# VectorE adds the scaled down product to the rows in four feed-forward units, in place of GpSimd, with the five engines' orders written anew behind the head

## The reference

```python
x = x + 0.5 * L0_ffn(layernorm(x))      # 704 hidden, integer weights with scales s_gate, s_up, s_down, silu
x = x + L0_attn(layernorm(x))           # 16 heads of 16, rotary, causal
x = x + 0.5 * L0_ffn(layernorm(x))
x = x + 0.5 * L1_ffn(layernorm(x))      # ternary weights, sigmoid gate
x = x + L1_attn(layernorm(x))           # 16 query heads, 4 key heads, linear position bias, causal
x = x + 0.5 * L1_ffn(layernorm(x))
```

## Time and profile before

| | us |
|---|---|
| median of 3 runs (lowest, highest) | 552.77 (552.47, 553.46) |
| the profiled execution | 552.14 |
| its span, first to last instruction | 550.4 |
| PE, DVE busy | 530.6, 456.1 |
| ACT, POOL busy | 401.3, 340.8 |

### The profile page before, as it was taken

One profiled execution on the slowest core, in us unless ns is written; L12 is line 12 of the kernel. 1 busy time (PEld: TensorE's weight loads), 2 busy tenths in 40 slices (PEclk: granted clock), 3 DMA queues, 4 the chain that ended last, 5 costly groups with the idle time before them and its releaser, 6 DMA issues.

```text
span 550.4 us, 12977 instructions
## 1 busy us (share of the span) xinstructions
PE 530.6 (96%) x5060; PEld 302.9 (55%) x5060; DVE 456.1 (83%) x816; ACT 401.3 (73%) x603; POOL 340.8 (62%) x427
## 2 busy tenths in 40 slices
PE   8999798999999999999899999999999999999997
PEld 6676444445554654566446564465455654654664
DVE  5999999998989797699987969879997779783363
ACT  5978594878777698775886848788769676969443
POOL 2549896975987797673664364552855626545634
PEclk9999999999999999999999999999999999999999
DMA  8900110302130100410110120010211011101211
GB/s 324 355 1 2 58 58 2 116 23 62 41 103 18 43 1 2 157 42 20 63 43 2 42 83 22 22 43 6 75 36 43 1 42 64 52 2 62 80 58 38
DMA packets 22573, 31.76 MB, mean 58 GB/s; under 512 B 9408, under 2 KB 10816, under 8 KB 22360
## 3 DMA queue, kind: packets, MB, share of 16 engines
q1 hardware_dynamic: 22512, 30.94, 16.4%
HBM read 13.75 MB, written 2.36 MB: 29 GB/s over the span
## 4 chain that ended last, share of the span: by engine, by line
PE 71%; DVE 17%; ACT 4%; issue 3%; POOL 2%; SPq 1%; DMA 0%; DVEq 0%; POOLq 0%; ACTq 0%
PE PS L597 22%; PE PS L621 12%; PE PS L708 10%; PE PS L688 5%; PE PS L673 5%; DVE MX L1064 5%; PE PS L639 4%; PE PS L723 4%; PE PS L580 3%; PE PS L544 2%; PE PS L559 2%; ACT PB L850 2%; PE PS L655 2%; DVE MX L1060 1%; DVE ST L875 1%
## 5 line engine op out<-in xcount | busy, mean ns | idle before, releaser
L850 ACT ACTIVATE PB<-PS 128x1024 f32<-128x1024 f32 x160 | 158.7, 1025 | 52.9 <-PE PS L688 48.4
L1064 DVE TENSOR_REDUCE MX<-PS 128x2 f16<-128x1024 f32 (+2 forms) x192 | 158.3, 865 | 13.8 <-PE PS L544 13.1
L597 PE MATMUL PS<-XT,WGU 128*128 128x512 f16 x660 | 156.9, 380 | 4.6 <-DVE QF L1042 3.0
L1140 POOL TENSOR_TENSOR HH<-TH,HH 128x512 f16<-128x512 f32 x71 | 82.5, 1173 | 69.0 <-ACT HH L818 69.0
L1168 POOL TENSOR_SCALAR_AFFINE_SELECT PB<-PB 128x512 f32<-128x512 f32 (+1 forms) x140 | 73.8, 552 | 48.1 <-ACT PB L850 47.9
L597 PEld LDWEIGHTS PS<-XT,WGU 128*128 128x128 f16 x660 | 59.6, 98 | 75.9 <-issue 7.8
L621 PE MATMUL PS<-WD,HH 128*128 128x256 f16 x660 | 78.2, 273 | 0.4 <-POOL HH L1140 0.2
L708 PE MATMUL PS<-PB,V 128*32 128x512 f32 (+3 forms) x1024 | 75.3, 435 | 0.8 <-ACT PB L850 0.3
L621 PEld LDWEIGHTS PS<-WD,HH 128*128 128x128 f16 x660 | 62.6, 98 | 13.3 <-issue 3.3
L818 ACT ACTIVATE HH<-TH 128x512 f16<-128x512 f32 (+1 forms) x86 | 52.9, 628 | 20.2 <-PE PS L621 6.9
L673 PE MATMUL PS<-SK,SQ 63*128 63x256 f16 (+3 forms) x512 | 59.5, 299 | 5.3 <-DVE MX L1064 2.6
(11 more groups left out here) (119 smaller groups left out, 777.7 us busy)
## 6 DMA issues: line engine op xcount, KB each, us to landing
SQ<-QPB SPq DMA_DIRECT2D x24, 256.0 KB, 2.5
OC<-OT SPq DMA_DIRECT2D x16, 256.0 KB, 2.4
RB<-scratch SPq DMA_DIRECT2D x64, 64.0 KB, 2.3
SK<-QPB SPq DMA_DIRECT2D x12, 256.0 KB, 2.4
SQ<-MT SPq DMA_DIRECT2D x128, 1.0 KB
out<-X SPq DMA_DIRECT2D x8, 256.0 KB, 2.1
PB<-gu SPq DMA_DIRECT2D x2, 704.0 KB, 6.1
LATE<-gu SPq DMA_DIRECT2D x2, 704.0 KB, 14.5
```

The lines of the kernel that those rows point to most:

```text
L597: m = e.matmul(o[:, :], WGU[l][:, k, col:col + P], rows_of(f)[j][:, k, :], start=j == 0 and k == 0, stop=j == 1 and k == 1)
L850: e.activation(PB[Q % 2][:, j, :, :], two_banks("s", i), ACT.Exp, scale=0.25).then_inc(a_exp, 1)
L1064: e.tensor_reduce(mx[:, :, pr, t], o[:, :, col:col + (t + 1) * P], AX.X, ALU.max, negate=True).then_inc(a_max, 1)
L1140: e.tensor_tensor(hh[1][:, s * T:(s + 1) * T], value_of(j)[0], hh[0][:, s * T:(s + 1) * T], ALU.subtract).then_inc(f_lo, 1)
```

## The change

In the units 4, 6, 8 and 10 DVE's step `d` gets a second instruction: behind the product into `DS` it waits for its own `f_ds` and adds `DS` to the two tiles of X, raising `f_res[0]`. POOL's string loses the eight `d` of these units; the first eight, of units 0 to 3, stay. All five orders and the banks are new from some point on (PE's from the 115th letter, DVE's from the 106th, ACT's from the 91st, POOL's from the 58th, SP's from the eighth), the head before is kept. PE, ACT and SP have the same letters as before, only in another sequence. The strings of DVE, ACT, POOL and the banks are left out here; around unit 6 DVE's is the same as before (`m d m m d m m x N m m m m m`), around unit 8 `d m d m N m m m o` has become `m d o l d N m m m m o`, with `d` here for the whole step.

```diff
--- before.py
+++ after.py
@@ -108,44 +108,44 @@
 
 ORDER = {
     "sp":
-        "kkrrkrkrDSrRDSRrrkDSkrRrDSRrrrkDSRkDSRrlrkkrDrSRrDSRrkklrDrSRrDSrRrkkrDrSRrDSRrDrkSkrDRSrRrrODSRDSOR"
+        "kkrrkrkDrSRrDSRrrkkrDSRrDrSRrDrSkRkDSRrrkklrDrSRrDlrSkRrkrDSRrDSrRrkkrrDrDSRSRrDrkkSRrDSrROrrDSORDSR"
         "OOOOOO",
     "pe":
         "zzzzzzzttzgGgggGGgGtzztgzGzagGgddddggGztzzgzGtGuugGaqqvgddgdvdqgGgqgtGGGguuGtqqqzmmmgmmgqmmdmmGsdsms"
-        "msdsmgmmsdsmmpmssgmsGsGsmspsmsgmmGmpsmssmsgmmsGmmpsmsvmsvsmsmuummpqssqosmoomssoddsmqqmspttmsdgggsGdG"
-        "smgmmspmsGmsmgsgsmGGmpmsvsmsddmsvumsdudqqsspmmoottoosmsggqsgmmgGgsGGsmpmsgmssqGttGpsssddssgddGgpmmgg"
-        "gGGmmmvgvmGuuGoooommsqsmqsmmqdmsdsmmddsmsmssmmspmmsmttsspsmgGggGGssmggGgGsmmpmtdtddssdsmggmspsmmgvGg"
-        "uugGsmqqgGsmsqGGoommspsmdddmsdmssoosmmmpmttsssgggmsGGsspmmgsmgGsmGGsmgsmpmsmvmddmssdsmsdmsspmsttooos"
-        "mmogguuGgGsqmmsqgqGsmgGgGmmspsmsdsmsdmmsddsmpmsmsmsmpsttvmsggGgsmsGgGgGgGsmtmmsddtddsmppmsouooougmsm"
-        "qsgqssqgssGGsspmsmgmGmmpmmmvgGmsgsmsGsmsttmmpssgdsmmdddoooosmsgGgmmsGmmpssgssGggssspssGGttpgGggddddG"
-        "ggGgGGooooddddttgggGgGGgGGgdddd",
+        "msdsmgmmsdsmmpsmsgmsGsGmsspmsgmsGmmmpssmssgmsmGmmpssmvmsvsmsummumpqmsqossooosdsdqmmsqptsmtdmggdgsGsG"
+        "smgmmspmsGsmgmssgmGmGpsdmsmdvmsvmssduudqmsqspmoomsttosogGggmsqGmggsGmspmsqsmgsGtGtpsssdgsdsgddGpmmGg"
+        "gmGmGggvmmuGvmooouosmqmsqsmmqdmsdmmdsdsmsmssmmspmsmmttsspmsggGgGsmmgGgGgGttsmpssmdddsmsdggmspmsmgGvg"
+        "GusmguGgGqssGqmsmpmsdmmsdqdoodsmsosmmompmttsssgsggGGsmpsmmgsmgGsmgsmGGmmspmsmvddsmsdsmdssmpsmstoomst"
+        "oomggguGuGsqmsmqgqmsggGGGmsmpsmdmsdmsmdsdsmspsmssmmmspttvsmggGgGgGmsgGsgGsmmtmsddsmmddsspptououoogsm"
+        "qmsqsqggGssGsspmsmgmGmmpmmmggvmsGsmsGsmtsmtmpsmsdsmsddgdoooomsgmsgGGmmmpssGssgggssspsstGGtpGggdgdddG"
+        "ggGGGgoooodddttdggGgGggGGGgdddd",
...
@@ -1026,6 +1026,10 @@
                                                o.rearrange("p (t n) -> p t n", t=2), 0.5 / HS,
                                                SD[:, :].unsqueeze(1).to_broadcast([P, 2, D]), ALU.mult,
                                                ALU.mult).then_inc(f_ds, 1)
+                        if f >= NB:
+                            w.wait_ge(f_ds, 2 * before(f, 0) + pair + 1)
+                            xv = X[:, NT * b + 2 * pair:NT * b + 2 * pair + 2, :].rearrange("p t n -> p (t n)")
+                            e.tensor_tensor(xv, xv, DS[:, :], ALU.add).then_inc(f_res[0], 1)
                     else:
                         xv = X[:, NT * b + 2 * pair:NT * b + 2 * pair + 2, :].rearrange("p t n -> p (t n)")
                         e.scalar_tensor_tensor(xv, o, 0.25 / XS, xv, ALU.mult, ALU.add).then_inc(f_res[1], 1)
```

More of the change, by code:

```diff
@@ L125 @@
[L125 to L128, removed]
-    "act":
[L130 to L135, removed]
+        "mdmkmhsnmhmxmshmcmmmmxsmmmhmcmxmmmuumpmqpoxqoNdmpmqpqmttmxshsksdhhmmcmsmhmmxsmhshmnmmcxmdmuudNqmpqmp"
@@ new lines @@
+        "mottxoNhhmhmpqkhmmmxhcphttqdshsdnhmmcksmhsmshsmhxmmhuoumomlmmllxmdmmdmmxNmmmmmttNmhhxhmkhmhchtmmxtdm"
+        "dnssmhmkshmhscmuxushshhlmmlmmxmdoldNmmmmomttxNhhhmckmmmxhmmhhmmmxcmdmmdmnmomttxmoshsuhushlmkmlslmshx"
+        "shhmmmmdmxmdmNmmNmmxttmhchhkmhchhmmtxmdmmdnuotumhmlxlklhohNcmmmmmxhmmmmhmchxmtmmtmmxdhdoomNmhmmmxhkh"
+        "cththhchdkdhhhohoNXdtthdhhkhhhdd",
+    "act":
+        "wXxxTwttthtXhhthxxhtwwhtthwXthwtxwthYyyxthkhhkkvwQttQXtktvkhtYQyytQhhhxxkkkhhtwTQteQeeeetehQhweoeeet"
+        "eQheeoetehoeeeeteYhoeeveveecyyhoceeeeeQeQXxxeQtQtohteeetheoeheteehthcheoeYveeeyyveceXoexxettQtehQhXe"
+        "httehoeeethxxQhoeeeetQethoYththttvccyhvyehQeQheQeeeeeeeoXexxeeetothtXhethhttxehhoexeceetteohetYhtvet"
+        "yhythQeeQhheoeceQeeeXoxxeeeettthehoetethetehhheocevXeeeeecoeexexYttytyhehQehtQQetthheheoeeeeeoeeeXeo"
+        "xxvXttethhthethethehxecceeoYoyxyeteQhQeeQtteeheeoethoXttveheeexehxheeceeoctethethXoeeeteteeeeehhxxot"
+        "hohttcthhthchtthhXxxthtthhtthhth",
@@ L136 @@
     "pool":
-        "wwwrrhrhhhhddewhwhhhshasraqdqdseasaqqhhshahhswaqqsffasfadfqdqffhfhffwehfffcfhffChcCsfsaafrfqqssaaqqd"
-        "fffhdchfffhhhefdCfcdfrCsasfafrfqsqhahfffhhhsafqqffhceChcChfhhdffdfrffbrhhfffhhhcfffehChchCbhhdfdffrf"
-        "ffhfhcffrhhhCcfCehffhfbhhfhfdfdffrcrhhfhhhfcCfeCffffhfrfhbhhhcfcCCrffhffffffhchhhCchChhhhrhhhhh",
+        "wwwrrhrhhhhddewhwhhhshasraqdqdseasaqqhhshahhswaqqsffasfadqfdffqwhfffhfeffhcfhffcCChssaffrfaqqssaaqqd"
+        "fffdhfhffchhheffCfcrCsfsaarqhffqhfshaffshhqfaffqcehhcCChhfhffrffffrhhffhhhfcffCehhhhhcCfffrbfffhbfhc"
@@ L141 @@
+        "ffrhhhCcCfefhhfhhfhbfffffrrhhhhhcfcfCfCefffhfffrhhchhCcfCffrfhffbfffhhchhChchChhhrhhhhh",
     "banks":
         "1224635601407234516352416761235476510274367165037426041260721525067436517265226046201624620662462526"
-        "4206260426056240752042057305360246024502735203520630642016423510513013656240625345170215460270426130"
-        "6135026305320372054613046136741041657013650462063526016406430642063751630517342350235126302673021403"
-        "0642403604214626402406240625051370513157402175130643750273107624205460260325617450621430641376064202"
@@ L146 @@
-        "5436116351361064526045602745275103651365203705346134724064202407136570146342176043416056314064725042"
-        "0570242054205264026046345160435063257607506341601253750264276240735631041654025603502365036525027025"
-        "40264502720452062120537203610413463042672046032503464315275046357372145632576341240",
+        "4206260462056240725040572460427040625620735205373063057204530157642125323507064173167504650270426042"
+        "0653062306146026412573150213417103631570357460242532614602474134615423052735035053201653062735723054"
@@ L149 @@
+        "3165063604205316536406240642315370513502473240632103273502460230642164306423701253701652307642071406"
+        "4175461436461064526042560235735073520362043703523615064136404620643260526031245063461063417630124601"
+        "4720240642407420642064523603502167035265306430623605614574605361460263210264025613510463146031246024"
+        "60246052402652062516410615306413463042672046130512460313231047124545371623701430437",
 }
```

1 line of the change is left out of this document (removed).

## The result

The changed kernel takes **561.94 us** at the median, the kernel before 553.12 in the runs beside it: a ratio of 1.0152 (95% interval 1.0126 to 1.0177). One of the four executions behind the 561.94 took 888.64 us at a mean granted clock of 0.558; it is left out of the ratio, and the median of the other three is 561.37. The prediction was 555.0 us, in a range of 551.2 to 557.8. The sign was right. The size was +8.3 us (561.37 against 553.12) and +8.7 in the second set, in place of +2.2, outside the range.

What follows compares the result with a forecast made beforehand. PE was taken as the bound, 96% busy. Adds +0.9, changes of kind +2.6 and waits -1.3 gave +2.2 us on 552.8, so 555.0 us, range 551.2 to 557.8.

Steps and rivals of the forecast that it cites:

- What bounds the kernel: Whole span: PE, 96% busy with 71% of the chain; lengthening PE's stream costs in full, relieving POOL gives little.
- The adds: Units 4, 6, 8, 10: eight additions on DVE, 0.69 to 1.17 us each, cost +0.9 us (-0.5 to +3.3).
- Changes of kind: PE's switches between scores and full products: 298 in place of 270, about 0.105 us each, +2.6 us (+1.5 to +2.9).
- The waits: PE's 6.0 us of visible waits from 104 to 520 us: the new order wins back 1.3 us (-4.5 to +1).
- The one wait with a named cause: At 125 us SP issues RB's transfers before the denominators; DVE stands 1.17 us, PE 0.4; first denominator transfer now goes earlier.
- SP's k10 and k11: SP issues these behind S7 and r18: costs nothing, up to 1 us if k11 lands late.
- the tail: From 520 us on nearly unchanged, one down product moved behind the last unit's transposes: 0 (-0.3 to +0.4) us.
- the rivals: Alternatives for the whole kernel: waits emptied, 550.8 us (0.18); even, 552.8 (0.22); additions meeting POOL, some 557.5 (0.08).
- the port: Every addition meets a POOL instruction, takes 1.17 us and delays POOL's cuts: +7.3 us at most, some 557.5; chance 0.08.
- What would show it: Slower gate and down products at 128 to 266 us, p12 some 2 us later, additions of 0.69 us, POOL 10 us less busy.
- The signal that was to fell the forecast: PE's visible waits from 104 to 520 us shrinking from 6.0 us to under 2 would refute the prediction.

Runs made afterwards that it cites:

- second set: The changed kernel timed again, unaltered, in a second set of runs: 561.11 us against 552.42 for the kernel before.
- e2: Kernel before with only the eight additions moved from POOL to DVE, all other orders old: 556.61 us, ratio 1.0063.
- e7: Changed kernel's new orders with the additions kept on POOL, POOL's ninth `d` put ahead of `c3`: 560.58 us, ratio 1.0142.
- e1: The changed kernel as it is, repeated for an undisturbed profile: 561.11 us, ratio 1.0147 to the kernel before.
- e4: Kernel before with fourteen pairs of neighbours swapped in PE's order, 298 changes of kind in place of 270: 555.48 us, ratio 1.0058.
- e12: Changed kernel with five DVE and POOL instructions moved so that L1015's subtractions don't start during POOL's TENSOR_TENSOR: 560.05 us, ratio 1.0119.
- e9: Changed kernel, same orders, with 70 of the 683 PSUM bank choices made otherwise: 559.32 us, ratio 1.0112.
- e13: Changed kernel with both the 70 other bank choices and the five moved DVE and POOL instructions: 558.22 us, ratio 1.0096.
- e11: Kernel before with eleven PE products moved over one to three neighbours, 248 changes of kind in place of 270: 562.24 us, ratio 1.0157.
- e14_after_light_dve: Changed kernel with DVE's maxima taken over every second column of the scores only: 557.75 us, ratio 1.0067.
- e3_orders_only: Changed kernel's new orders with the additions kept on POOL, its ninth `d` behind `c3`: 566.56 us, ratio 1.0244.
- e15_before_light_dve: Kernel before with DVE's maxima taken over every second column of the scores only: 551.91 us, ratio 0.9988.

## Why the prediction was wrong

Its steps, in their order:

- **What bounds the kernel**: right. PE is 96% busy in both, and what came on top came on PE's stream and in its waits.
- **The adds**, taken at +0.9 us (-0.5 to +3.3): too small for the old order, in which they cost 2.8 us in the trace (e2), inside the range. By units: 4, taken at 0, was +0.9 through the meeting with POOL; 6, taken at +0.7, was +0.8; 8, taken at 0, was +0.4; 10, taken at +0.2, was +1.0, since "DVE has 1.7 us free" in a window of 12 does not say that they lie where the adds stand. Each add by itself was 0.69 us, as taken. The upper end of 1.17 us was too low: one took 1.56. In the new order they cost 0 to 0.5 us (e7 against e1).
- **Changes of kind**, taken at +2.6 us: right, 2.66 in the trace of the changed kernel, and e4 measured 2.65 in the trace and some 3 us in time.
- **The waits**, taken at -1.3 us (-4.5 to +1): this is the step that failed. The orders alone added 4.9 us (e7), far outside its bounds. The stated range did not even use the bound of +1: its upper end adds the adds' 3.3 and 2.9 for the changes to a saving of 1.3. With +1 it would have reached 560.0, still under what was measured. The one wait with a named cause did shrink: DVE's reciprocal waited 0.53 us for the denominators in place of 1.17,

```profile
132.88 0.35 DVE L1079 RECIPROCAL DC<-DC 128x32 f32<-128x32 f32 x1 [0.53 <-DMA DC<-OT]
```

  and PE's wait of 0.4 us behind it is gone. But at 121 to 125 us three others grew, by some 0.5 us together:

```profile
121.45 0.39 PE L688 MATMUL PS<-SQ,SK 64*128 64x384 f16 x4 [0.43 <-DVE MX L1064]
122.33 0.39 PE L673 MATMUL PS<-SK,SQ 63*128 63x384 f16 x4 [0.49 <-ACT PB L850]
...
125.09 0.39 PE L688 MATMUL PS<-SQ,SK 64*128 64x256 f16 x4 [0.42 <-ACT PB L850]
```

  The fault in the reasoning was to look only at the waits that the kernel had, for which a new order can be nothing but good. With 6 us of visible waits in 416, an order that fits this tightly has far more to lose than to win; the range should have been open on that side. Of these 4.9 us, moving the subtractions away from POOL took 1.2 (e12) and other banks 1.5 (e9), but both together only 1.9 (e13), since they remove some waits twice. For the other 3 us the places of most are known and the cause is not: 1.0 us from p11 to p12, 0.3 each from p2 to p4 and p15 to p17, 0.4 from p22 to p23, 0.3 in the tail. That a reader served later is dear is shown by e11; that it is what happened in these places is argued, not shown.
- **SP's k10 and k11**, the tail: nothing and +0.3 us, within what was given.
- **The sum against the rivals**: the port was one of them, with eight adds meeting POOL. It came, but by another instruction: one of eight adds was hit in the old order, and two less hard in the new one (1.22 and 0.89 us), while of the subtractions of L1015 behind the head five were, against one before. (Its "some 557.5" is also a wrong sum: with half of the 3.8 us on the path it is 558.2.) I had looked for it only at the instructions that the change adds, and not at those that it moves.
- **What would show it**: POOL 10 us less busy (9.4), its chain share the same, adds of 0.69 us with one over 1 us, gate products of 0.97 us: all seen. p12 came at 273.2 and not 2 us later than 266.1: of the 7.0 us, 2.1 are the head of this profile, 2.1 the changes of kind and 2.8 new waits. The signal that was to fell the forecast (visible waits under 2 us) was on the wrong side; they were 8.8.

## What to carry to other kernels

In a kernel whose busiest engine idles 1 to 2%, judge a new order first by what it can lose: each reader that gets its input later, and each instruction of two SBUF inputs that now starts inside one of GpSimd's. Price changes of kind on PE by the trace (0.1 us each here), but don't save them at the cost of the beat in which ACT and DVE are served: 22 fewer won 2 us and lost 11. And test an order apart from the edit that it came with; here the edit alone cost a third, and the order alone nearly all.

## What was not expected of the hardware

- **Stretches of half clock.** In e1_after PE stood 2.96 us at 66 to 69 us, and the granted clock was at its lower level, 1.2 in place of 2.4 GHz, from 68.7 us on for 3.4 us. The kernel before has the same stand at 65 to 68 us, and its clock stays full. Timeline of PE and windows (columns as above), first e1_after, then the kernel before:

```profile
69.14 1.44 PE L597 MATMUL PS<-XT,WGU 128*128 128x512 f16 x3 [2.96 <-DVE QF L1046]
68.70:72.10 3.40, 2.96 (x8) 1.07 (x9) 3.37 (x7) 3.30 (x7) 3.18 (x4) 0.50 0.00 0
...
68.28 1.02 PE L597 MATMUL PS<-XT,WGU 128*128 128x512 f16 x4 [2.96 <-DVE QF L1042]
68.70:72.10 3.40, 3.40 (x21) 2.08 (x20) 3.34 (x6) 3.19 (x7) 3.26 (x4) 1.00 0.00 0
```

  Four profiles have such a stretch inside the span, and each time it begins in the last half microsecond of a stand of PE or up to 1.4 us behind its end: e1_after and e14_after_light_dve (2.96 and 2.97 us of standing), e3_orders_only (2.74, clock 0.51 from 202.0 to 205.4) and e15_before_light_dve (2.30). Five more profiles than that of the kernel before have a stand of 2.95 to 2.97 us without it. So a stand of PE of 2.3 to 3 us can be followed by it and need not be; what decides is not shown. It falls on some executions of a kernel (3 of the first 12 of the kernel before) and not on others, so the times come in steps of 1.5 to 2 us.
- **Who holds the port.** Of two instructions with two SBUF inputs on DVE and POOL, the one that started first ran as if alone, and the other ended about 0.55 us after it (1.09 + 0.55 = 1.64, measured 1.63, at 214.09; 1.01 + 0.55 = 1.56 in e2's add). Being 0.1 us earlier is worth 0.9 us. But who goes next when POOL has a row of them is not settled by who started first: at 214.09 DVE went before POOL's next instruction, which took 1.58 us, while in e15 at 103.06 four POOL instructions that started after DVE's subtraction all went ahead of it and it took 4.04 us. POOL's causal cuts (L1168, one SBUF input) held it as well.
- **Less work on DVE, little gain.** 73 us less work on an engine that is busy 83% left the median of the kernel before where it was, since DVE, being earlier, met POOL for 4.04 us; with the same clock on both sides the gain was 2.4 us.
